# Graph network, attention stage: keys and queries of a chunk from one product with a block matrix, and the query bias in the type table

## What is computed

```
q = (x @ Wq + bq).reshape(n, nh, hd)          # nh = 4 heads of hd = 16
k = (x @ Wk + bk).reshape(n, nh, hd)
v = (x @ Wv + bv).reshape(n, nh, hd)
e_k, e_v = ek_tab[edge_type], ev_tab[edge_type]
logits = sum(q[dst] * (k[src] + e_k), -1) * scale + es_tab[edge_type] + log(eg_tab[edge_type])
attn = softmax of the logits over the edges with the same dst
agg = segment_sum((v[src] + e_v) * attn, dst)
```

## Time and profile before

| | us |
|---|---|
| three timed runs | 5319.16, 5328.72, 5332.62 |
| their median | 5328.72 |
| the profiled execution, its own time | 5317.69 |
| its span, first to last instruction | 5315.9 |
| of it the attention stage's chunks | 2440 to 3015 |
| TensorE busy in the whole span | 3389.1 |
| POOL busy | 3086.2 |
| VectorE busy | 2638.3 |
| ScalarE busy | 1088.7 |

### The profile page before, as it was taken

One profiled execution on the slowest core, in us unless ns is written; L12 is line 12 of the kernel. 1 busy time (PEld: TensorE's weight loads), 2 busy tenths in 40 slices (PEclk: granted clock), 3 DMA queues, 4 the chain that ended last, 5 costly groups with the idle time before them and its releaser, 6 DMA issues. The chain is left out here.

```text
span 5315.9 us, 58056 instructions
## 1 busy us (share of the span) xinstructions
PE 3389.1 (64%) x12064; PEld 2038.0 (38%) x12064; DVE 2638.3 (50%) x6534; ACT 1088.7 (20%) x2025; POOL 3086.2 (58%) x2552
## 2 busy tenths in 40 slices
PE   3654735555896788676898677776635555555524
PEld 1222534444675666452333244554412222222213
DVE  5997741111355322465666546666644444444423
ACT  0232411111122111122333223332311111111100
POOL 0374048887111881335676588888538888787740
PEclk7686655555555555555555555555557777777765
DMA  3122621111464110451111323333212222233210
GB/s 140 44 71 68 269 102 22 23 23 20 105 166 124 23 22 6 160 203 49 34 34 35 58 42 73 84 86 72 70 43 30 30 30 30 27 30 30 27 16 3
DMA packets 360442, 335.42 MB, mean 63 GB/s; under 512 B 268311, under 2 KB 297481, under 8 KB 360292
## 3 DMA queue, kind: packets, MB, share of 16 engines
q1 hardware_dynamic: 232910, 253.30, 15.1%
q0 software_dynamic: 114032, 67.92, 11.9%
q10 hardware_dynamic: 13350, 12.40, 0.7%
HBM read 172.92 MB, written 162.66 MB: 63 GB/s over the span
## 5 line engine op out<-in xcount | busy, mean ns | idle before, releaser
L843 PE MATMUL e_ps<-e_msg,e_hot 128*128 x2408 | 598.0, 425 | 325.8 <-POOL e_msg L754 231.4
L843 PEld LDWEIGHTS e_ps<-e_msg,e_hot 128*128 128x128 f32 x2408 | 539.4, 326 | 430.5 <-issue 430.5
L2269 POOL DMA_INDIRECT out<-d_out,d_end x356 | 592.0, 1663 | 172.1 <-issue 167.2
L1742 POOL DMA_INDIRECT u_a<-attended,dst_end x392 | 501.0, 1278 | 149.0 <-issue 117.4
L2313 PE MATMUL d_pl<-d_hot,d_fields 128*65 128x512 f32 x712 | 503.1, 872 | 0.0
L815 DVE TENSOR_TENSOR e_ps<-e_ps,e_before 128x65 f32<-128x65 f32 (+1 forms) x172 | 40.1, 233 | 792.5 <-PE e_ps L843 792.5
L2032 POOL DMA_INDIRECT list<-s_rec,s_place x200 | 199.3, 996 | 288.9 <-DVE s_place L1948 232.8
L735 POOL DMA_INDIRECT e_msg<-from_src,e_src x200 | 194.1, 970 | 286.3 <-DMA e_first<-lot_first 231.8
L1427 ACT ACTIVATE u_zt<-u_pt 128x256 f32<-128x256 f32 (+1 forms) x392 | 163.5, 433 | 615.6 <-PE u_pt L1327 615.4
L946 POOL DMA_INDIRECT a_ends<-h,a_src x200 | 201.5, 1007 | 146.7 <-DMA a_etype<-in_etype 93.7
L740 POOL DMA_INDIRECT e_msg<-h1d,e_src x200 | 221.4, 1107 | 102.7 <-issue 54.8
(11 more groups left out here) (370 smaller groups left out, 7910.4 us busy)
## 6 DMA issues: line engine op xcount, KB each, us to landing
u_z<-h SPq DMA_DIRECT2D x28, 896.0 KB, 6.3
x<-sums SPq DMA_DIRECT2D x28, 896.0 KB, 7.8
u_x<-x SPq DMA_DIRECT2D x28, 896.0 KB, 7.4
terms<-s_zeros SPq DMA_DIRECT2D x16, 812.5 KB
s_key_row<-src_key SPq DMA_DIRECT2D x50, 256.0 KB, 3.0
h1d<-u_h SPq DMA_DIRECT2D x14, 910.0 KB, 9.5
u_z<-h1d SPq DMA_DIRECT2D x14, 910.0 KB, 4.6
term<-u_h SPq DMA_DIRECT2D x14, 910.0 KB, 3.6
```

The source lines that it names most:

```text
L843: last = nc.tensor.matmul(to, hot[s][:, q, :], rows, start=False, stop=q == LOT - 1)
L1742: pool.indirect_dma_start(A[s][:, j, :], None, net.attended[:, :], bass.IndirectOffsetOnAxis(ap=net.dst_end[:, tile:tile + 1], axis=0)).th ...
L2269: pool.indirect_dma_start(net.out[:, :], bass.IndirectOffsetOnAxis(ap=end[s][:, j:j + 1], axis=0), out[s][:, j, 0:C], None, bounds_check=N ...
```

## The change

The weights of keys and queries go into one 128x128 block matrix `w_kq`, keys in the upper left block and queries in the lower right, with zeros elsewhere. One product with the turned features then writes the keys to partitions 0 to 63 and the queries to 64 to 127 of one bank. The type table gets 64 more columns that hold the query bias for each type, so the product with the one-hot adds it (each edge has exactly one type). ScalarE copies the queries without a bias.

```diff
-    net.wq = sb("wq", [P, C])
-    net.wk = sb("wk", [C, C])
+    net.w_kq = sb("w_kq", [P, P])
     net.wv = sb("wv", [C, CV])
-    net.bq = sb("bq", [C, 1])
-    net.tabs = sb("tabs", [3 * NET, C + 2 * CV], BF16)
+    net.tabs = sb("tabs", [3 * NET, P + 2 * CV], BF16)
...
-        types = sb("types", [NET, C + 2 * CV])
+        types = sb("types", [NET, P + 2 * CV])
...
-                (net.wq[C:, :], d["L2_gnn_Wq"][:, :]), (net.wk[:, :], d["L2_gnn_Wk"][:, :]),
+                (net.w_kq[0:C, 0:C], d["L2_gnn_Wk"][:, :]), (net.w_kq[C:P, C:P], d["L2_gnn_Wq"][:, :]),
                 (net.wv[:, 0:C], d["L2_gnn_Wv"][:, :]),
-                (net.bq[:, :], d["L2_gnn_bq"][:, None]),
+                (types[:, C:P], d["L2_gnn_bq"][None, :].to_broadcast([NET, C])),
...
                 nc.vector.memset(net.w_lin[:, :], 0.0)
+                nc.vector.memset(net.w_kq[:, :], 0.0)
...
-                    nc.tensor.matmul(pq[0:C, :], net.wq[C:P, :], feat[C:P, :], start=True, stop=True)
-                    nc.tensor.matmul(pk[0:C, :], net.wk[:, :], feat[0:C, :], start=True, stop=False)
-                    nc.tensor.matmul(pk[0:C, :], net.tab_k, oht[:, :], start=False, stop=True).then_inc(projected, 1)
+                    nc.tensor.matmul(pk[:, :], net.w_kq[:, :], feat[:, :], start=True, stop=False)
+                    nc.tensor.matmul(pk[:, :], net.tab_kq, oht[:, :], start=False, stop=True).then_inc(projected, 1)
...
-                    nc.scalar.activation(qs[:, :], pq[0:C, :], ACT.Identity, bias=net.bq[:, :]).then_inc(qs_ready, 1)
+                    nc.scalar.activation(qs[:, :], pk[C:P, :], ACT.Copy).then_inc(qs_ready, 1)
```

More of the change, by code:

```diff
@@ L88, in allocate @@
     net.w_lin = sb("w_lin", [P, P])
-    net.wq = sb("wq", [P, C])
-    net.wk = sb("wk", [C, C])
+    net.w_kq = sb("w_kq", [P, P])
     net.wv = sb("wv", [C, CV])
-    net.bq = sb("bq", [C, 1])
-    net.tabs = sb("tabs", [3 * NET, C + 2 * CV], BF16)
-    net.tab_k, net.tab_v, net.tab_l = net.tabs[:, 0:C], net.tabs[:, C:C + CV], net.tabs[:, C + CV:C + 2 * CV]
+    net.tabs = sb("tabs", [3 * NET, P + 2 * CV], BF16)
+    net.tab_kq, net.tab_v, net.tab_l = net.tabs[:, 0:P], net.tabs[:, P:P + CV], net.tabs[:, P + CV:P + 2 * CV]
     net.head_sum = sb("head_sum", [C, CV])
@@ L138, in prepare @@
         leg = sb("leg", [NET, NH])
-        types = sb("types", [NET, C + 2 * CV])
-        type_rest = sb("type_rest", [NET, C + 2 * CV])
-        type_parts = [sb(f"type_part{i}", [NET, C + 2 * CV], BF16) for i in range(3)]
+        types = sb("types", [NET, P + 2 * CV])
+        type_rest = sb("type_rest", [NET, P + 2 * CV])
+        type_parts = [sb(f"type_part{i}", [NET, P + 2 * CV], BF16) for i in range(3)]
         gb = sb("gb", [1, 2 * C])
@@ L230, in _ @@
                 nc.vector.memset(net.eps[:, :], EPS)
-                nc.vector.memset(types[:, 2 * C:C + CV], 1.0)
+                nc.vector.memset(types[:, P + C:P + CV], 1.0)
                 nc.vector.tensor_tensor(types[:, 0:C], ek[:, :], bk[:, :], ALU.add)
-                nc.vector.tensor_tensor(types[:, C:2 * C], ev[:, :], bv[:, :], ALU.add)
+                nc.vector.tensor_tensor(types[:, P:P + C], ev[:, :], bv[:, :], ALU.add)
                 v.wait_ge(film_done, 1)
@@ L262, in _ @@
                 v.drain()
-                nc.vector.tensor_copy(types[:, C + CV:2 * C + CV].rearrange("e (h d) -> e h d", d=HD),
+                nc.vector.tensor_copy(types[:, P + CV:P + C + CV].rearrange("e (h d) -> e h d", d=HD),
                                       es[:, :].unsqueeze(2).to_broadcast([NET, NH, HD]))
-                nc.vector.tensor_copy(types[:, 2 * C + CV:], es[:, :])
+                nc.vector.tensor_copy(types[:, P + C + CV:], es[:, :])
                 left = types
@@ L888, in attention_sums @@
         dsum = sb("dsum", [P, J, NH])
-        pt, po, pg, pq, pk, pv, pl, pr = map(ps, (
-            "features", "types", "starts", "queries", "keys", "values", "logit", "sums"))
+        pt, po, pg, pk, pv, pl, pr = map(ps, (
+            "features", "types", "starts", "keys_queries", "values", "logit", "sums"))
         loaded = [sem(f"loaded{s}") for s in range(2)]
```

## The result

| | median us | runs | lowest to highest |
|---|---|---|---|
| kernel before | 5319.78 | 20 | 5309.45 to 5332.62 |
| kernel after | 5339.96 | 20 | 5328.72 to 5351.41 |

The changed kernel is slower: the ratio is 1.0039, with a 95% interval of 1.0031 to 1.0048. That is 20.2 us. The profiled execution of after took 5342.56 us, 24.9 more than that of before.

A forecast was written before the change was run, and what follows sets the result against it. The prediction took TensorE's ordered queue in the attention stage's 50 chunks as the bound. From the profiled 5317.69 us, +5.0 (product), -1.0 (type product), +0.4 (preparation) and +16.5 (clock) gave 5338.6 us; range 5309 to 5360.

The forecast's parts named there:

- the clock's term: Attention stage: chunks partly run at 2.4 GHz (raised) fall from 15 to 8 of 50, 2.35 us each, +16.5 us.
- The product: Key and query product in the attention stage: two 128x128 passes take 2.00 us against 1.90, +5.0 us over 50 chunks.
- The type product: Product with the one-hot, 128 columns for 64: -0.02 us a chunk, -1.0 us in all.
- The query bias: ScalarE's copy of the queries without bias saves 0.08 us a chunk off the path, so nothing in time.
- The table loads: ScalarE's 24 function table loads of 1283 ns, one in every second chunk, stay: no change.
- The preparation: Ahead of the stage: a 128x128 clearing and six operations widened from 8x200 to 8x264, +0.4 us.
- The chunk's length: Attention loop: a chunk longer by 0.08 us is 0.8 us off after ten, so the repeating pattern of high-clock chunks is lost.
- the first regime's rate: From 2445 to 2660 us, 3 of 18 chunks reach the high clock; applied to all 50 it gives 8.
- No chunk is raised: Rival: the merged product never raises the clock in the attention stage, +35.3 us, 5357 us; sign under 5 raised; chance 0.20.
- More are raised: Rival: the full-size product raises the attention stage's clock more easily, 25 of 50 chunks, 5299 us; chance 0.15.
- Raises stay at 15: Rival: the count of high-clock chunks in the attention stage does not change, 5322 us; chance 0.12.
- The table loads vanish: Rival: ScalarE's 24 table loads go with the changed function, 21 us less than the forecast, 5317 us; chance 0.03.

The follow-up runs named there:

- the first experiment: Kernel before with the values' weights padded from 68 to 96 columns of zeros, pair of products untouched; 5336.84 us against 5313.78, ratio 1.0037.
- the second: Kernel after with the merged product split again into two 64x64 products writing halves of one bank, wide type table kept; 5337.26 us, ratio 1.0041.

## Why the prediction was right, point by point

The forecast of 5338.6 us is 1.4 below the measured 5339.96. That it came so close is luck: the clock's term was 7.0 us too small, and other terms and the spread of single executions made up for most of it. What held is the direction and that the clock, not the product, carries the change.

- **The product**: +0.10 us a chunk forecast, +0.07 to +0.08 measured (1.97 and 1.98 for 1.90), within the bounds. (The planner's three passes in the earlier trace rows are the first three of line 370, whose fourth the view cuts off, and not the last three of a product; their distance of 0.85 us is read rightly.) The pair did run as one product, and the merge saved nothing. The row of 128 by 128 float32 loads shows 311 ns, that of 64 by 68 203 ns: 108 ns more, which is not all hidden. The Trainium skill, "TensorE: Matmul & The Clock Gate", section "LDWEIGHTS (loading the stationary operand)", gives columns over 1.2 in ns, which is 50 ns for these 60 columns; this trace shows twice that for float32, so the measurement decides.
- **The type product**: -0.02 us forecast and -0.03 measured from its start to that of the starts, with records of 603 ns for 629 and 99 ns for its load.
- **The query bias** is gone from ScalarE's copy (594 ns) and gave nothing, as forecast: TensorE doesn't wait for VectorE's product in any chunk of after. **The table loads** are the same 24. **The preparation**: the stage began 0.9 us earlier, not 0.4 later, less than two executions differ by.
- **The chunk's length** came to +0.05 us, not +0.08. This small error did no harm, because the clock's term didn't hang on its size: by the prediction's argument any length off 11.87 loses the pattern.
- **The clock**: 15 to 8 raised chunks and +16.5 us forecast; 15 to 5 in the profiled execution, +23.5, and 3 in another. The direction held, and so did the cause as far as it goes: a chunk longer by 0.05 us loses rises with the pair in place (the first experiment); for a shorter chunk it is shown in part (the second). The mis-sized step is "I take the first regime's rate: 3/18". Nothing tied that rate to another length: before had it at 11.87 us itself, its second trace has 5 of 18 there, and after has 3 of its 5 raised chunks in its first 18. It gave 8, where the kernels with an altered chunk showed 3 to 10 in 50. The clock's term was 7.0 us too small. The chunks' length was 1.8 too large (4.0 for 2.2) and the preparation 1.3. The rest of the gap lies in single executions: the profiled one of after is 2.6 us above its median, that of before 2.1 below its own, so the medians are 20.2 apart where the profiled executions are 24.9, and the forecast added 20.9.
- **The measure of no change**: here the text missed. It set the sum against 5328.72, the median of three runs, and so called its forecast +0.2%. Against the 5319.78 of twenty runs, near which the profiled execution lies, it is +0.35%, and +0.39% was measured. The prediction took 0.3% as what can be told from no change and gave no change the largest chance, 0.48; the measured interval, 1.0031 to 1.0048, is clear of 1. The sum stood on the right number, the chances on the wrong one.

**The rivals.** "No chunk is raised", for want of two products at once, fell: 5 and 3 chunks are raised behind the merged product, and the wider values' product lost as many rises with the pair in place. By the prediction's own sign, fewer than 5 raised, the trace with 3 would have spoken for this rival; the 4 with the pair in place take that away. "More are raised" fell with 5 and 3 of 50. "Raises stay at 15" fell by the same count; only with the unread products do both kernels have the same number, 43. "The table loads vanish" fell with the 24 that stayed.

**What stays open.** That a chunk of 11.87 us fits some pattern of the rises was argued from their repetition. It agrees with the longer chunks (3 to 5 raised for 15) and less well with the shorter one (10), and nothing here shows what such a length would have to fit. Nor do the runs show what in a stretch of work raises the clock, or what made before's executions differ by up to 34 us on one chip.

## What to carry to other kernels

Two products that already run at once on different rows are one product in time, so look for the overlap in the timeline before you merge them. Where TensorE is the bound and shows 1.2 GHz between short rises, a change of a few hundredths of a microsecond can move the time by 0.4%; here a longer and a shorter chunk both cost that. Price such a change by the rises it may lose, and try unread products in TensorE's waits first, which was worth 0.8% here and left no difference between the two kernels that could be measured. Compare with many runs of before, since three can lie 9 us off.

## What the runs showed that was not expected

- Added work made the kernel faster: four unread products a chunk, with records of 0.43 to 0.55 us each, took 46.6 us off (5321.16 to 5274.59) by a granted clock of 0.77 where it was 0.55 in before. The Trainium skill, "TensorE: Matmul & The Clock Gate", Part 1, says that activity releases the throttle; with this the runs agree. But TensorE's 519 busy us of 575 at a clock of 0.51 in after show that in this stage being busy was not enough.
- The place of four small products changed a chunk by 0.23 us with the same work (11.87 to 11.64).
- Two products at once may write the two halves of one PSUM bank, and take the same 1.90 us as with two banks.
- Float32 weights of 96 columns took 249 ns to load and of 68 203 ns, 1.6 ns more for each further column, and the product behind them grew by 0.05 us:

```profile
L988 PEld LDWEIGHTS a_values<-a_feat,wv 64*96 64x96 f32 x94 | 17.9, 249 | 17.7 <-issue 17.7
```
